# Who normalises: moving value times inverse root plus shift from VectorE to ScalarE in a four-layer decoder kernel

## The reference, cut to what matters

```python
def _layernorm(x, axis=-1, eps=1e-05):
    m = jnp.mean(x, axis=axis, keepdims=True)
    v = jnp.var(x, axis=axis, keepdims=True)
    return (x - m) / jnp.sqrt(v + eps)
...
    x = _layernorm(x + _L3_ffn_ref(x, ...), axis=-1)
```

## Time and profile before

| what | value |
|---|---|
| median of three runs | 2705.77 us (2696.03 to 2719.74) |
| the profiled execution | 2701.65 us |
| its span | 2699.8 us, 1.85 us less than its time |
| mean granted TensorE clock | 0.847 |
| busy: PE, DVE, ACT, POOL | 80%, 61%, 44%, 24% of the span |

### The profile page before, as it was taken

How to read it: one execution, slowest core, us unless ns; L and a number is a source line. 1 busy time by engine, 2 the same in 40 slices (tenths; PEclk the granted TensorE clock), 3 DMA queues, 4 the chain that set the end, 5 groups by cost and what they waited for, 6 DMA issues and landing times. The chain is left out here.

```text
span 2699.8 us, 44010 instructions
## 1 busy us (share of the span) xinstructions
PE 2171.9 (80%) x15402; PEld 1103.4 (41%) x15402; DVE 1640.8 (61%) x3606; ACT 1191.1 (44%) x2185; POOL 641.1 (24%) x817
## 2 busy tenths in 40 slices
PE   2899999976899997759999888629587774777778
PEld 1233455433233343635554444328422221345556
DVE  4788676568787642456666554235566774346666
ACT  0377766542377652214665675404232210533333
POOL 4211111124211010432121112144136663100000
PEclk9699999876599995767999999659798875778899
DMA  3300111000101010621111000039400001011111
GB/s 125 109 25 25 39 35 33 25 15 26 34 25 31 15 27 1 196 84 37 37 32 35 20 21 16 13 121 304 135 0 1 0 1 39 18 55 55 48 63 48
DMA packets 105916, 132.99 MB, mean 49 GB/s; under 512 B 25078, under 2 KB 89398, under 8 KB 105059
## 3 DMA queue, kind: packets, MB, share of 16 engines
q1 hardware_dynamic: 94580, 112.48, 13.8%
q10 hardware_dynamic: 7344, 9.92, 1.1%
q0 software_dynamic: 3776, 7.79, 0.8%
HBM read 70.65 MB, written 13.49 MB: 31 GB/s over the span
## 5 line engine op out<-in xcount | busy, mean ns | idle before, releaser
L1519 DVE TENSOR_REDUCE maxima<-psM 128x2 f32<-128x1024 f32 (+4 forms) x640 | 678.4, 1081 | 321.1 <-PE psM L1196 134.4
L1383 ACT ACTIVATE probs<-psE 128x512 f32<-128x512 f32 (+2 forms) x1248 | 699.6, 584 | 390.3 <-PE psE L1219 186.7
L1219 PE MATMUL psE<-q_stack,k_stack 53*128 53x512 bf16 (+3 forms) x1152 | 371.7, 360 | 41.4 <-ACT probs L1383 31.0
L1196 PE MATMUL psM<-k_stack,q_stack 51*128 51x512 bf16 (+3 forms) x1280 | 356.6, 351 | 14.2 <-DVE maxima L1519 7.6
L2346 DVE SCALAR_TENSOR_TENSOR hres<-psM,gates,hres 128x128 f32<-128x128 f32 x512 | 144.1, 344 | 84.0 <-PE psM L2280 83.1
L1219 PEld LDWEIGHTS psE<-q_stack,k_stack 53*128 53x128 bf16 x1152 | 97.5, 94 | 225.9 <-ACT probs L1383 145.4
L1196 PEld LDWEIGHTS psM<-k_stack,q_stack 51*128 51x128 bf16 x1280 | 100.8, 97 | 185.7 <-issue 98.8
L1667 POOL TENSOR_SCALAR pool_t<-mean_var 128x4 f32<-128x4 f32 x60 | 14.6, 243 | 652.0 <-DVE mean_var L1444 645.1
L2280 PEld LDWEIGHTS psM<-values,probs 128*128 128x128 f32 x1024 | 137.7, 196 | 60.1 <-issue 59.6
L1239 PE MATMUL psB<-probs,values 128*32 128x256 f32 (+3 forms) x1696 | 157.2, 443 | 2.4 <-ACT probs L1383 1.7
L1130 PE MATMUL psE<-masks_bf,ident_bf 64*128 64x128 bf16 (+2 forms) x960 | 153.9, 245 | 0.0
(11 more groups left out here) (416 smaller groups left out, 3741.6 us busy)
## 6 DMA issues: line engine op xcount, KB each, us to landing
q_stack<-q_parts SPq DMA_DIRECT2D x432, 64.0 KB
values<-experts_dram SPq DMA_DIRECT2D x40, 514.0 KB, 4.7
values<-experts_dram SPq DMA_DIRECT2D x32, 512.0 KB, 3.3
k_stack<-k_parts SPq DMA_DIRECT2D x156, 64.0 KB
hid<-experts_dram SPq DMA_DIRECT2D x15, 514.0 KB, 4.6
work<-experts_dram SPq DMA_DIRECT2D x15, 514.0 KB, 4.7
pack<-pack_dram SPq DMA_DIRECT2D x1, 4647.0 KB
work<-sorted SPq DMA_DIRECT2D x70, 65.0 KB, 3.6
```

What stands on the lines that cost most here:

```text
L1196: out, len(heads), keys, lo, max_mask(c, t), lambda i, to, start, stop: nc.tensor.matmul(to, q_stack[lo:lo + R_MAX, job.a % Q_SLOTS, pair_ ...
L1219: lambda h, to, start, stop: nc.tensor.matmul(to, ks[lo:lo + R_END, pairs[h], k * P:k * P + c.kn], q_stack[lo:lo + R_END, job.a % Q_SLOTS, ...
L1383: nc.scalar.activation(probs[0:c.kn, m % 2, heads[0]:heads[-1] + 1, q0:S], psE[0:c.kn, n % 2, 0:len(heads) * (S - q0)].rearrange("p (h q) ...
L1519: nc.vector.tensor_reduce(top, psM[:, at:at + len(banks), 0:per * keys].rearrange("p b (h k) -> p b h k", h=per), AX_X, ALU.max, negate=Tr ...
```

## The change: normalisation on ScalarE

ACT gets a task "post_n" in each job, and it takes "post_c" over from DVE. Each issues 4 ACTIVATE instructions with the function Identity, `scale=roots` and `bias=shifts` (both one value per partition). POOL's "root" makes the shift with two more instructions. DVE keeps "post_b" only where there is a gain and shift ("twice" and "tail"); there it now waits for ACT (`normed`). PE's "back" waits for `normed`, or for `gained` after a "twice". "quant_a" gets a wait for `normed`, since its input is written by ACT. The planner gets lengths for the new tasks, and root's goes from 2.8 to 3.2.

```diff
@@ class Plan
-        self.put(t + 4.0, "post_b", job)
+        self.put(t + 3.6, "post_n", job)
+        if job.post in ("twice", "tail"):
+            self.put(t + 4.6, "post_b", job)
...
-            return [] if job.kind in ("load", "unload") else [("post_c" if job.post == "tail" else "post_b", x)]
+            return [] if job.kind in ("load", "unload") else [
+                ({"tail": "post_c", "twice": "post_b"}.get(job.post, "post_n"), x)]
...
-            return 2.8 if task == "root" else 1.3 if task == "k_split" and not x.att.wide else 3.8
+            return 3.2 if task == "root" else 1.3 if task == "k_split" and not x.att.wide else 3.8
...
@@ PE
-                                pe.wait_ge(turn_ready, turned_no[job])
+                                if job.post == "twice":
+                                    pe.wait_ge(gained, gained_no[job])
+                                else:
+                                    pe.wait_ge(normed, turned_no["post_c" if job.post == "tail" else "post_n", job])
...
@@ ACT
+                        elif task in ("post_n", "post_c"):
+                            u, part = job.u, 1 if job.kind == "quantized" or task == "post_c" else 0
+                            src = yt if task == "post_c" else {"norm": xt, "inner": hres, "inner2": hres}.get(job.post, yt)
+                            to = xt if task == "post_c" or job.post in ("std", "mlp") else yt
+                            act.wait_ge(root_done, plan.roots[job, part] + 1)
+                            for t in range(QT):
+                                last = nc.scalar.activation(to[:, u, t, :], src[:, u, t, :], ACT.Identity,
+                                                            bias=shifts[:, u, t:t + 1], scale=roots[:, u, t:t + 1])
+                            last.then_inc(normed, 1)
...
@@ DVE
-                    def normalise(job, part, out, src):
-
-                        u = job.u
-                        dve.wait_ge(root_done, plan.roots[job, part] + 1)
-                        for t in range(QT):
-                            me.mark(nc.vector.tensor_scalar(out[:, t, :], src[:, t, :], mean_var[:, u, t, 0:1],
-                                                            roots[:, u, t:t + 1], ALU.subtract, ALU.mult))
-                        me.wait()
...
+                            dve.wait_ge(normed, turned_no["post_c", plan.before[job]])
...
-                            normalise(job, part, to[:, u], src[:, u])
+                            dve.wait_ge(normed, turned_no["post_n", job])
...
-                            normalise(job, 1, xt[:, job.u], yt[:, job.u])
-                            dve.sem_inc(turn_ready, 1)
...
@@ POOL
-                            nc.gpsimd.tensor_tensor(y, y, t, ALU.mult).then_inc(root_done, 1)
+                            me.mark(nc.gpsimd.tensor_tensor(y, y, t, ALU.mult))
+                            me.wait()
+                            me.mark(nc.gpsimd.tensor_tensor(t, mean_var[:, u, :, 0], y, ALU.mult))
+                            me.wait()
+                            nc.gpsimd.tensor_scalar(shifts[:, u, :], t, -1.0, None, ALU.mult).then_inc(root_done, 1)
```

More of the change, by code:

```diff
@@ L432, in needs @@
             return [("quant_b", x)]
+        if task == "post_n":
+            return [("root", x, 1 if job.kind == "quantized" else 0)]
         if task == "post_b":
-            return [("root", x, 1 if job.kind == "quantized" else 0)]
+            return [("post_n", x)]
         if task == "post_c":
@@ L470, in engines @@
             return ("POOL",)
-        if task in ("k_evac", "v_evac", "o_copy", "turn_evac", "back_evac", "gelu"):
+        if task in ("k_evac", "v_evac", "o_copy", "turn_evac", "back_evac", "gelu", "post_n", "post_c"):
             return ("ACT",)
-        if task in ("q_evac", "rq_evac", "rk_evac", "split", "share", "mix", "quant_a", "quant_b", "quant_c", "post_a", "post_b",
-                    "post_c"):
+        if task in ("q_evac", "rq_evac", "rk_evac", "split", "share", "mix", "quant_a", "quant_b", "quant_c", "post_a", "post_b"):
             return ("DVE",)
@@ L547, in length @@
             return {"post_a": {"norm": 1.6, "mlp": 3.1}.get(x.post, 2.4) if task == "post_a" else 0.0,
-                    "post_b": {"twice": 2.8, "tail": 5.0}.get(x.post, 1.4) if task == "post_b" else 0.0,
+                    "post_b": 1.5 if task != "post_b" or x.post == "twice" else 3.7,
                     "q_evac": 0.8, "rq_evac": 2.3, "rk_evac": 2.3, "split": 0.5, "share": 0.7, "mix": 0.7, "quant_a": 1.7,
-                    "quant_b": 3.6, "quant_c": 4.0, "post_c": 1.4, "k_split": 2.2 if task != "k_split" or x.att.wide else 1.0}[task]
+                    "quant_b": 3.6, "quant_c": 4.0, "k_split": 2.2 if task != "k_split" or x.att.wide else 1.0}[task]
         if engine == "ACT":
             short = {"k_evac": 0.33, "v_evac": 0.26} if task in ("k_evac", "v_evac") and not x.att.wide else {}
-            return short.get(task, 2.0 if task == "gelu" else 0.6)
+            return short.get(task, {"gelu": 2.0, "post_n": 1.25, "post_c": 1.25}.get(task, 0.6))
         if engine == "POOL":
-            return 2.8 if task == "root" else 1.3 if task == "k_split" and not x.att.wide else 3.8
+            return 3.2 if task == "root" else 1.3 if task == "k_split" and not x.att.wide else 3.8
         return 0.0
@@ L763, in build @@
         pool_t = sb("pool_t", [P, 2, QT])
+        shifts = sb("shifts", [P, B, QT])
         peak = sb("peak", [P, B, 2, QT])
@@ L1024, in segment @@
             turned_no = {}
+            gained_no = {}
             for item in plan.order["DVE"]:
-                if item[0] == "post_c" or (item[0] == "post_b" and item[1].post != "tail"):
-                    turned_no[item[1]] = len(turned_no) + 1
+                if item[0] == "post_b" and item[1].post == "twice":
+                    gained_no[item[1]] = len(gained_no) + 1
+            for item in plan.order["ACT"]:
+                if item[0] in ("post_n", "post_c"):
+                    turned_no[item] = len(turned_no) + 1
             turn_before = {j: atts[j.a - 1] if j.a else None for j in atts}
@@ L1057, in segment @@
                            kc_moved0_0, kc_moved0_1, kc_moved1_0, kc_moved1_1, kc_moved2_0, kc_moved2_1, max_split,
-                           rows_moved0, rows_moved1, stats_done, root_done, turn_ready, quant_ready, gelu_done,
+                           rows_moved0, rows_moved1, stats_done, root_done, normed, gained, quant_ready, gelu_done,
                            w_moved, own_dve, own_pool):
@@ L1606, in _ @@
                             u = job.u
-                            part = 1 if job.kind == "quantized" else 0
-                            src = {"norm": xt, "inner": hres, "inner2": hres}.get(job.post, yt)
-                            to = xt if job.post in ("std", "mlp") else yt
-                            normalise(job, part, to[:, u], src[:, u])
+                            dve.wait_ge(normed, turned_no["post_n", job])
                             if job.post == "twice":
                                 gain_shift(yt[:, u], "g2", "b2")
-                            if job.post == "tail":
+                                dve.sem_inc(gained, 1)
+                            else:
                                 gain_shift(yt[:, u], "g3", "b3")
```

5 lines of the change are left out of this document (1 added, 4 removed).

## The result

The changed kernel takes 2735.96 us (median of 4 runs, 2735.48 to 2739.13), the kernel before 2706.89 us (4 runs, 2696.03 to 2719.74). The ratio is 1.0116, 95% interval 1.0078 to 1.0153: it is slower by 29 us by the medians and by some 31 us by the ratio, and lies above the range that I gave. Its profiled execution took 2739.13 us with a span of 2737.2 us.

A forecast was written before the change was run, and what follows sets the result against it. PE was taken to bound most of the kernel, DVE the middle from 575 to 653 us. Middle -11.4, collided calls -3.4, serial places +6.0 and full parts +3.3 gave -5.5 on 2701.65: 2696 us, range 2676 to 2724.

The forecast's parts named there:

- What bounds the kernel: Whole kernel: PE bounds most places, DVE's own list the stretch from 575 to 653 us, a serial chain the stretch ends.
- My term of -11.4: Middle, 575 to 720 us: DVE relieved of normalisations gains 11.4 us, bounds 0 and -18.8.
- The marker: End of the DVE-bound stretch: the keys' split of L1a in unit 0 comes 5 to 12 us earlier.
- The price of a call: Each normalisation on ACT: four ACTIVATEs take 1.52 us, bounds 1.16 and 1.82, against 1.11 on DVE.
- the two calls of 3.78 us: DVE calls at 554.96 and 1646.05 us: moved to ACT, they save 3.4 us together, bounds 0 and -4.5.
- The serial places: Six normalisations with nothing beside them: each ends 1.0 us later, +6.0 us, bounds 3.7 and 7.6.
- The longer root: POOL's root: two dependent steps end each root 0.56 us later, charged at serial places and unit 0's middle chain.
- a rival of 7.3 us in the middle: Root chain, middle: 13 roots push each other, losing 7.3 of 11.0 us; 2704 us, chance 0.18.
- The full attention parts: 33 calls between exps: 0.1 us each, +3.3 us, ends 0 and 0.4 (+13).
- ACT's list is held: Full parts: ACT waits for a root with exps behind it, PE stands; 1 us a call, 2726 us, chance 0.13.

The follow-up runs named there:

- e2: Changed kernel with ACT normalising (longer root) only in L0c, linear and quantized, DVE with the short root elsewhere: 2681.6 us, ratio 0.9893 to the kernel before.
- e4: Changed kernel's task structure, but every normalisation on DVE with the short root: 2694.3 us, ratio 0.9950 to the kernel before.
- e9: e5 without its two extra root passes, still planned with 3.2 for a root: 2699.4 us, ratio 0.9990 to the kernel before.
- e14: e5 with the two extra passes only in the 20 roots of L0c, linear and quantized, same order: 2705.5 us, ratio 1.0008 to the kernel before.
- e15: e5 with the two extra passes only in the 40 roots outside L0c, linear and quantized, same order: 2713.4 us, ratio 1.0033 to the kernel before.
- e5: e4 with two extra POOL passes in every root, planned with 3.2, all normalisations on DVE: 2724.1 us, ratio 1.0066 to the kernel before.
- e11: Changed kernel, planner starting ACT's normalisation 1.6 us later in attention L1a alone: 2714.0 us, ratio 1.0044 to the kernel before.
- e8: e4 plus a stand-in in ACT's list at 56 places, four ACTIVATEs without the wait for the root: 2725.1 us, ratio 1.0069 to the kernel before.
- e7: e4 plus a stand-in in ACT's list at 56 places, only the wait for the root: 2701.1 us, ratio 0.9977 to the kernel before.
- e3: Changed kernel with ACT normalising in all jobs but L0c, linear and quantized, which use DVE and the short root: 2729.3 us, ratio 1.0086 to the kernel before.
- e16: Changed kernel, same order, with the shift computed beside the root's steps: 2726.5 us, ratio 1.0091 to the kernel before.
- e17: Changed kernel, planner starting ACT's normalisation 1.6 us later in the second stretch alone: 2725.2 us, ratio 1.0072 to the kernel before.
- e1: Changed kernel, planner starting ACT's normalisation 1.6 us later everywhere, no instruction changed: 2705.1 us, ratio 0.9988 to the kernel before.
- e18: Changed kernel, planner starting ACT's normalisation 1.6 us later in all jobs but L0c, linear and quantized: 2711.9 us, ratio 1.0028 to the kernel before.
- e12: e2 planned with 2.8 for a root and the shift computed beside the root's steps, passes in all 60 roots: 2696.9 us, ratio 0.9977 to the kernel before.
- e10: e5 planned with 2.8 for a root, keeping the two extra passes: 2718.7 us, ratio 1.0060 to the kernel before.

## Why the prediction was wrong, step by step

**What bounds the kernel** was read rightly. The full parts are PE's, the middle was DVE's: with ACT in the middle alone the last exp of L1a.0 comes 17 us earlier than before. e2 is 0.0057, 15 us, faster than e4 (the same lists from the second stretch on) and 0.0097, 26 us, faster than e9; both have no normalisation on ACT. My term of -11.4 with its bound of -18.8 was right in sign and too small. The marker that I named for it was a bad one. I wrote that the keys' split of L1a in unit 0 would come 5 to 12 us earlier than 652.66; it came later, and yet L1a began 11.3 us earlier:

```profile
656.89 0.43 DVE L980 CAST k_parts<-work 128x512 bf16<-128x512 f32 x1 [0.25 <-DVE yt L1473]
```

No more work stands ahead of it in DVE's list: it holds the same number of maxima, measures and steps of "quantized" as before, without the normalisations. What grew are DVE's waits for others, from 2.1 to 15.8 us in 575 to 653 us. So DVE had set the stretch as a whole, and this instruction did not mark its end.

**The price of a call** was 1.65 us, not 1.52: 478 ns for one, 114 ns more than the 364 ns of the form with one pointer, and not the 90 ns seen on 128x512. That form read PSUM and this one reads SBUF, so the runs don't say whether the pointer or the operand makes the other 24. It stayed under my bound of 1.82, and no ACTIVATE of the 224 took over 496 ns, so the two calls of 3.78 us are gone as I had counted. The Trainium skill, "ScalarE: Activation LUTs", section "What ACT_TABLE_LOAD costs", gives 186 ns and 0.833 ns an element, 93 ns for each pointer, and an overlap of 93 ns; for 128 elements an estimate by that page is 479 ns and 1.64 us a call, and the trace agrees (478 ns, 1.65 us).

**The serial places** held where I looked: at the end of the first stretch it is 3.73 us from the root's first pass to PE's transposes before, and 4.81 now (1077.39 to 1082.20), 1.08 us more against my 1.0.

**The longer root** was right by the instruction (0.56, measured 0.60) and wrong by the place. I charged it to six ends and to four roots of one chain, 5.6 us, and kept a rival of 7.3 us in the middle. Passes alone cost 21 to 30 us, by e14 and e15 more of it outside the middle than in it. My reason against was that DVE waits only 1.3 us for GpSimd. That row says who waits at the place where it arrives, not what the delay does afterwards. In e5 it came back as PE's clock; by what path from a root to PE stays open.

**The full attention parts** are the step that failed most. I took 0.1 us a call with an upper end of 0.4, from a gelu that kept ACT from exps for 3.4 us and PE for 0.86. In 180 to 480 us that holds: PE's waits there grew from 6.6 to 10.0 us, as I had written (under 12). In L1a it fails. Three waits stand there in front of calls, two of 1.59 us and one of 0.82, and PE stopped for 2.06, 2.06 and 2.14 us; L1a costs 15 to 19 us in all, by the exps of three executions, since the clock fell with the stops. The work alone is cheap there: 1.6 us in all with the late start (e11), 1.8 more in e8 than in e7. So by these runs it is the wait and the work in a row that PE could not bridge. The rival "ACT's list is held" had this mechanism to the letter, down to psE and two exps. I gave it 0.13 because "the planner allows 3.2 us for a root, which is 2.6 + 0.56 in the trace". The root did last 3.08 us. What came late was its start: DVE's measure ended at 785.02, the root began at 785.11, and ACT had done all that stood ahead of the call at 786.63, 1.59 us before it could go. And I priced a stop at its own length. A term for a stop of PE at granted clock 1.00 needs a second part for the matmuls behind it, and I had the rows for it: the earlier trace rows show 50.98 us of PE busy at 0.50 with only 152 matmuls.

**What I had not priced.** The new tasks alone, with nothing moved, made it 13 us faster (e4, interval 5 to 22 us). A changed order had no term in my sum. Nor had the work between exps, for which I allowed no more than 0.4 us a call with the wait in it: 56 stand-ins without a wait cost 25 us (e7 to e8), 0.45 us each.

From before over e4, e9 and e5 to the changed kernel the ratio goes by -0.005 (tasks), +0.004 (planned with 3.2), +0.0076 (passes) and +0.005 (DVE to ACT). These four make +0.0116 by the way they are taken, and each is good to 0.004. The last hides two of opposite sign, -0.0115 in the middle (e14 to e2) and +0.0053 elsewhere (e15 to e3), which together make -0.006 and not +0.005. The orders of these pairs differ too.

The gap does not lie at the start of L1a, though the changed kernel's own trace suggests it. From the last exp of L0s.3 to that of L1a.0 the kernel before takes 253.6 us and e2 236.7. The changed kernel takes 246.8, but e11, e16 and e17, whose lists are the same up to there, take 237.4, 237.3 and 237.4. So the move to ACT gained 16 us in the middle with everything moved as with the middle alone, and the profiled execution of the changed kernel lost 10 us there to its clock (0.71 on average, against 0.73 to 0.75 in the other three). What was lost lies behind it: 15 to 19 us in L1a, and more from L2c.1 to L2x.3. There the changed kernel, e3, e11 and e16, with the same lists, take 279 to 298 us, the runs with a late start 276 to 279, and before and e4 265 and 266. So the late start is worth some 10 us there, and longer roots and the work between exps remain, in shares that stay open. Open is also why e1 and e18 lose 7 and 10 us against the kernel before between L1a.3 and L2x.3.

## What to carry to other kernels

Before work is moved into the list of an in-order engine that feeds PE, ask what the moved instruction waits for and what stands behind it; put it late rather than early, as a late start of 1.6 us was worth up to 31 us here with no instruction changed, only the order. Look also at what stands between the exps even without a wait: 1.65 us of work at 56 places cost 25 us. Price a stop of PE in a full stretch by the clock it loses, and look for that in PE's busy time for the same number of matmuls, not in the waits. Move only the part that relieves the bound engine: the middle alone on ACT ran at 2681.6 us, against 2706.9 before and 2736.0 with everything moved.

## What the hardware showed that I had not expected

Executions of one kernel differ by the granted clock of TensorE, before any normalisation of an attention has run. In the 20 profiled executions the last exp of L0a.0, which no edit touches, ends between 160.3 and 173.4 us. e2 and e12 have the same order of instructions up to L0c.3, near 590 us, and no root before 160 us. From 60 to 165 us they read (e2, then e12):

```profile
60.00:165.00 105.00, 87.32 (x494) 22.91 (x494) 77.23 (x89) 46.58 (x83) 17.66 (x20) 0.76 0.25 84
```

```profile
60.00:165.00 105.00, 89.53 (x417) 21.80 (x416) 69.85 (x81) 39.09 (x69) 17.66 (x20) 0.63 0.24 81
```

The second is 9 us behind at the end of the first attention part, and 9 to 11 us up to the end of L1a. The same three stops of PE in L1a went with some 31, 24 and 17 us at the lower level in the changed kernel, e16 and e17 (0.92, 0.94 and 0.95 over the whole stretch). The executions of e10 reach from 2698 to 2738 us, and its profiled one (2698.08) shows none of the loss that its median has. So one profile against another tells a mechanism, but not a size below some 10 us; the sizes above are from medians, of 4 runs for the changed kernel and 6 to 12 for the others.
